# A four-layer graph network on one core: TensorE's updates sent by drains, and GpSimd's gathers issued in pairs behind a count of written ones

## The reference

```python
h = relu(layernorm(x)); x = x + L0(h)   # agg = segment_sum(h[src], dst); MLP 256-512-256, two batch norms
h = relu(layernorm(x)); x = x + L1(h)   # a_in = segment_sum((h@W_in+b)[src]*w, dst)
                                        # a_out = segment_sum((h@W_out+b)[dst]*w2, src); gates: sigmoid, tanh
h = relu(layernorm(x)); x = x + L2(h)   # agg = segment_sum(w*h... [src], dst); MLP 256-256-256, two batch norms
h = relu(layernorm(x)); x = x + L3(h)   # msg = relu([x_i, x_j-x_i]@W1+b1)@W2+b2 per edge; mean over the edges
```

## Time and profile before

| | |
|---|---|
| timed runs, median (lowest to highest) | 3428.49 us (3427.81 to 3428.86) |
| profiled execution, span | 4205.1 us |
| profiled span less timed median | 776.6 us |
| PE matmul busy | 2930.9 us, 70% |
| DVE busy | 2117.9 us, 50% |
| ACT busy | 1141.1 us, 27% |
| POOL busy | 2373.5 us, 56% |
| POOL gathers and scatters, lines 834, 860, 810 and 945 | 1170, 391, 400 and 440 |
| granted TensorE clock, mean | 0.826 |

### The profile page before, as it was taken

One profiled execution on the slowest core, in us unless ns is written; L12 is line 12 of the kernel. 1 busy time (PEld: TensorE's weight loads), 2 busy tenths in 40 slices (PEclk: granted clock), 3 DMA queues, 4 the chain that ended last, 5 costly groups with the idle time before them and its releaser, 6 DMA issues. The chain is left out here.

```text
span 4205.1 us, 55362 instructions
## 1 busy us (share of the span) xinstructions
PE 2930.9 (70%) x11580; PEld 1849.8 (44%) x11581; DVE 2117.9 (50%) x6459; ACT 1141.1 (27%) x3023; POOL 2373.5 (56%) x2458
## 2 busy tenths in 40 slices
PE   3677776555542846677588887755554899988989
PEld 1233333333321434444333332433333548888878
DVE  6566664333320455444456655533333576667664
ACT  1466661000000330000000000300000356666662
POOL 3544445666667046666666666666666226666662
PEclk6788887667665867888799999976676999999999
DMA  3000002333320043333366666433333136666664
GB/s 123 2 1 1 1 1 74 90 89 90 90 56 2 20 139 88 101 106 105 109 176 180 177 176 178 138 89 89 87 91 86 34 124 186 187 188 185 189 187 143
DMA packets 184321, 438.94 MB, mean 104 GB/s; under 512 B 53924, under 2 KB 78623, under 8 KB 184233
## 3 DMA queue, kind: packets, MB, share of 16 engines
q0 software_dynamic: 135568, 372.32, 31.3%
q1 hardware_dynamic: 48665, 65.55, 4.7%
HBM read 403.39 MB, written 34.24 MB: 104 GB/s over the span
## 5 line engine op out<-in xcount | busy, mean ns | idle before, releaser
L834 POOL DMA_INDIRECT acc<-table,stg_idx x1170 | 1128.5, 965 | 767.8 <-issue 349.1
L2116 PE MATMUL psum<-acc,oh 128*128 x2600 | 871.4, 489 | 637.7 <-issue 456.5
L2116 PEld LDWEIGHTS psum<-acc,oh 128*128 128x128 f32 x2600 | 598.2, 244 | 912.3 <-issue 821.2
L1497 DVE TENSOR_TENSOR acc<-acc,psum 128x257 f32 (+1 forms) x660 | 276.0, 418 | 962.7 <-remote 565.4
L1032 ACT CAST stg_idx<-rec 128x2 int32 (+1 forms) x784 | 148.4, 193 | 2113.0 <-remote 841.2
L945 POOL DMA_INDIRECT TT<-qtable,stg_row x440 | 424.1, 964 | 282.4 <-PE psum L2428 150.9
L860 POOL DMA_INDIRECT H<-gtable,stg_idx x391 | 379.1, 970 | 199.5 <-issue 116.5
L2205 PE MATMUL psum<-H 125*128 125x440 bf16 x1600 | 375.5, 399 | 154.2 <-issue 48.2
L2137 PE MATMUL psum<-H,oh 128*128 x880 | 426.2, 630 | 79.8 <-issue 31.1
L810 POOL DMA_INDIRECT recs<-acc,sst_idx x290 | 284.6, 981 | 338.1 <-ACT acc L977 255.6
L2428 PE MATMUL psum<-oh,TT 128*128 128x128 f32 x3520 | 444.3, 277 | 34.7 <-issue 26.0
(11 more groups left out here) (277 smaller groups left out, 3210.7 us busy)
## 6 DMA issues: line engine op xcount, KB each, us to landing
acc<-table,stg_idx POOLq DMA_INDIRECT x1173
TT<-loc_dram SPq DMA_DIRECT2D x22, 320.0 KB
TT<-qtable,stg_row POOLq DMA_INDIRECT x440
Wm<-loc_dram SPq DMA_DIRECT2D x22, 320.0 KB
H<-gtable,stg_idx POOLq DMA_INDIRECT x391
gtable<-H SPq DMA_DIRECT2D x24, 256.0 KB
qtable<-H SPq DMA_DIRECT2D x24, 256.0 KB, 2.2
table<-H SPq DMA_DIRECT2D x8, 640.0 KB
```

The lines of the kernel that those rows point to most:

```text
L834: pool.indirect_dma_start(out=dst[:, c, 0:D], out_offset=None, in_=src, in_offset=bass.IndirectOffsetOnAxis(ap=stg_idx[:, c:c + 1], axis=0 ...
L1497: V.tensor_tensor(at, at, sum_bank(j)[:, 0:w], ALU.add).then_inc(added, 1)
L2116: last = mm(sum_bank(j)[:, 0:w], oh[:, 2 * j + k, :], rows_flat[:, ds(start[j] + k * S, w)], start=(k == 0), stop=(k == 1))
```

## The change

Two things are changed, and each is small in code.

First, TensorE's updates. Where the last matmul of a group of products added to a semaphore, a drain behind it now adds to it. This holds for `used` in the placing phase (400 times), for `summed` in passes 0 to 3 (220 times each) and for `filled` in the four dense stages z0, up0, down0 and back0 (81 times). The other stages' banks, `spread` and pass 4's `summed` stay with the matmul.

Second, GpSimd's gathers of passes 0 to 3. Each of them now also adds one to a new semaphore, `written`, when GpSimd has written its descriptors (`engine_sem`). Before a pair is issued, GpSimd waits until all but the last two of the gathers before it have been written. The scatters have no such wait.

```diff
+WRITES = 2 * (GROUPS - 1) + 1
+BESIDE_SCATTERS = ("z0", "up0", "down0", "back0")
...
+            def pair_before_written(g, n):
+
+                pool.wait_ge(written, g * 2 + (2 - n * (2 * GROUPS - WRITES)))
+                pool.sem_inc(stages_begun, 1)
+
-            def gather_pair(i, j, src, dst):
+            def gather_pair(i, j, n, src, dst):
 
                 pool.wait_ge(staged, i * RING_G + j + 1)
                 pool.sem_inc(stages_begun, 1)
+                pair_before_written(i * RING_G + j, n)
                 for c in (2 * j, 2 * j + 1):
                     pool.indirect_dma_start(
                         out=dst[:, c, 0:D], out_offset=None, in_=src,
-                        in_offset=bass.IndirectOffsetOnAxis(ap=stg_idx[:, c:c + 1], axis=0)
-                    ).then_inc(landed[j], 16)
+                        in_offset=bass.IndirectOffsetOnAxis(ap=stg_idx[:, c:c + 1], axis=0),
+                        engine_sem=written).then_inc(landed[j], 16)
...
+            pool.sem_inc(written, 4)
...
             def done(ins, st, k):
-                ins.then_inc(filled[bank(st, k)], 1)
+                if st in BESIDE_SCATTERS:
+                    nc.tensor.drain().then_inc(filled[bank(st, k)], 1)
+                else:
+                    ins.then_inc(filled[bank(st, k)], 1)
...
-                    last.then_inc(summed, 1)
+                    nc.tensor.drain().then_inc(summed, 1)
...
-                    last.then_inc(used, 1)
+                    nc.tensor.drain().then_inc(used, 1)
```

More of the change, by code:

```diff
@@ L411, in gnn_kernel @@
         stages_begun = sem("stages_begun")
+        written = sem("written")
         zero_filled = sem("zero_filled")
@@ L842, in gathers @@
                     for j in range(RING_G):
-                        gather_pair(i, j, src, dst)
+                        gather_pair(i, j, n, src, dst)
                 for j in range(RING_G - 1):
-                    gather_pair((n + 1) * GITS - 1, j, src, dst)
+                    gather_pair((n + 1) * GITS - 1, j, n, src, dst)
                 pool.wait_ge(staged, (n + 1) * GITS * RING_G)
                 pool.sem_inc(stages_begun, 1)
+                pair_before_written((n + 1) * GITS * RING_G - 1, n)
                 c = 2 * RING_G - 2
@@ L850, in gathers @@
                     out=dst[0:END_ROWS, c, 0:D], out_offset=None, in_=src,
-                    in_offset=bass.IndirectOffsetOnAxis(ap=stg_idx[0:END_ROWS, c:c + 1], axis=0)
-                ).then_inc(landed[RING_G - 1], 16)
+                    in_offset=bass.IndirectOffsetOnAxis(ap=stg_idx[0:END_ROWS, c:c + 1], axis=0),
+                    engine_sem=written).then_inc(landed[RING_G - 1], 16)
             def gather_wide(g, j, half):
@@ L857, in gather_wide @@
                 pool.sem_inc(stages_begun, 1)
+                pair_before_written(g + 2 * GROUPS, 2)
                 r = END_ROWS if half else P
@@ L861, in gather_wide @@
                         out=ring_rows[0:r, c, :], out_offset=None, in_=gtable,
-                        in_offset=bass.IndirectOffsetOnAxis(ap=stg_idx[0:r, c:c + 1], axis=0)
-                    ).then_inc(landed_w[j], 16)
+                        in_offset=bass.IndirectOffsetOnAxis(ap=stg_idx[0:r, c:c + 1], axis=0),
+                        engine_sem=written).then_inc(landed_w[j], 16)
             def gathers_wide():
```

## The result

The changed kernel takes 4319.72 us (median, 4312.87 to 4326.72) against 3428.15 us (3426.13 to 3428.86) of before: a ratio of 1.2604, 95% interval 1.2589 to 1.262. The prediction was 3475.5 us with a range of 3230 to 3550, so the sign was the likelier one and the size was wrong by 844 us.

A forecast was written before the change was run, and what follows sets the result against it. The bound changes by stage: GpSimd's gathers in passes 0 to 3, with TensorE's updates held in the profile but likely not in timed runs. Drains add 33 + 9 + 5 = 47 us to 3428.5, giving 3475.5 us, range 3230 to 3550.

The forecast's parts named there:

- the sign: Whole kernel: slower was given 0.50, same 0.16, faster 0.34.
- Holds at the timed speed: Held TensorE updates beside GpSimd's descriptor trains: likeliest none in the timed runs, so 0 us to gain.
- 667 us of holds: Holds summed in the profiled execution: passes 338 us, late scatters 132, placing 197.
- The rival with real holds: Holds also exist in timed runs, so the change ends faster: 3268 us in the middle, 3085 at the end; chance 0.34.
- The argument that a recording makes them: Holds read as mainly a cost of being profiled: 0.70 us steps on idle register operations, timed runs 776.6 us shorter.
- The `written` wait: GpSimd's wait before each gather pair in passes 0 to 3: covered by the pair before, 0 us.
- Drains in the placing phase: 400 drained columns: TensorE's column grows from 0.73 to 0.90 us against VectorE's 0.816, costing 33 us, bounds 0 to 72.
- 1.1 dear: Marker for the profile after: placing columns 0.9 us apart as forecast, 0.82 for covered drains, 1.1 for dear ones.
- Around the late scatters: Drains on 56 banks of up0, down0 and z0 at 0.166 us each: 9 us, upper bound 21.
- Drains on sums: 220 drains per pass: 0 us in passes 0, 1 and 3, 5 us in pass 2, bounds 0 and 13.
- 1.19 us per gather: GpSimd's most per gather in timed runs; 8.9 gathers make 10.6 us per iteration, against TensorE's 11.1 with drains in pass 2.
- drains are dear, TensorE becomes the bound: Rival: a drain of 0.40 us costs 191 us over placing, pass 2 and late scatters, 3620 us; chance 0.09.

The follow-up runs named there:

- r1: The kernel before, unchanged, run and profiled again for a second trace: 3428.61 us, span 3426.9 us.
- v2: The changed kernel with the updates of the sums in passes 0 to 3 back on their matmuls, all else kept: 3623.32 us, ratio 1.056.
- s1: The kernel before with a drain behind each of the 880 sums of passes 0 to 3, nothing else: 4118.61 us, ratio 1.2023.
- v1: As s1, plus ten unread 128x128 matmuls at the start of each iteration in passes 0 and 3: 3846.31 us, ratio 1.1215.
- s4: The kernel before with a drain behind only the fifth sum of each iteration in passes 0 to 3: 3443.79 us, ratio 1.005.
- s3: The kernel before with a drain behind sums 1 to 4 of each five in passes 0 to 3: 3815.27 us, ratio 1.1135.
- e3: The kernel before with drains behind only the 81 banks of z0, up0, down0 and back0: 4281.09 us beside 4260.53, ratio 1.0053.
- s: Group of four runs with drains or halts on the sums of passes 0 to 3; the before beside them took 3428.07 us.
- t: Group of four runs (sums with filler, placing drains, `written` wait, drains on even columns); the before beside them took 4267.84 us.

## Why the prediction was wrong, step by step

- **Holds at the timed speed: 0.** Right (r1), and with it the bound: passes near 495 us each. The 667 us of holds are real differences between the two traces of before: 336 us in the passes, 135 around the late scatters, 218 in the placing phase, and 84 in pass 4 that the sum had left out. The rival with real holds (0.34) fell. The argument that a recording makes them fell too: the 0 is right, its reason was wrong, and the agreement is in part luck. No run shows what makes the steps of 0.70 us: the register operations of line 2137 are at 3 to 709 ns in the first trace of before and at 46, smallest and largest alike, in r1's. Profiled, r1 took 3428.61 us, no more than the seven runs of before beside it (3428.66 to 3431.28).
- **The `written` wait: 0.** Right: 0.30 us before each gather in v2.
- **Drains in the placing phase: 33 us, bounds 0 to 72.** 171 measured. The step that failed is what followed from "A drain ends the overlap, since nothing behind it starts before the tail is over". The sentence holds, and the 0.90 us with it (each of the 400 drains ends 20 to 23 ns behind the last matmul's recorded end in the changed kernel's trace), but as a price it is incomplete: I counted the 166 ns tail and at most a weight load. Behind the drain stand the column's register operation, its wait and the issue of its first load as well, 0.32 us that used to be done ahead. The column of 1.22 us is beyond the "1.1 dear" of my markers.
- **Around the late scatters: 9 us, at most 21.** 21 measured in v2, the same omission: four banks of up0 are 9.8 us apart from the next four, where r1 has 7.7.
- **Drains on sums: 5 us in pass 2, 0 elsewhere.** 217, and 94, 158 and 184 elsewhere (s1). This is the term that broke the forecast, and it failed twice. "In passes 0, 1 and 3 TensorE has time to spare", put at 0, took the idle time of the earlier trace rows as free. Part of it was where the sequencer prepared the next sums, two register loads of 1.24 us an iteration among it, and behind a drain none of the loads ran beside matmuls in passes 0 and 3 (0 us of them in the changed kernel, 34 and 36 of 95 in r1). In pass 2, by its rows, this is most of the loss, though no run sets it apart. And the step took TensorE's clock as given: in pass 3 the share granted fell from 0.74 to 0.51, and v1, with the same drains and a clock of 0.99, loses 2 us there instead of 184. For pass 1 the shares of the two stay open. The sum for pass 2 also had GpSimd's side too short: the 1.19 us per gather from the room in the timed runs is 1.26 in r1, so its limit is 11.2 us an iteration and not 10.6; by the prediction's own 11.1 for TensorE its 5 us would have been 0.
- **The rival "drains are dear, TensorE becomes the bound"** (0.09, 3620 us) had the right mechanism. It priced a drain at 0.40 us, where a column of the placing phase grew by 0.49 (0.73 to 1.22), but counted no register loads, no clock, and only 25 iterations of one pass. With 0.5 us a sum and 3.0 us of bare loads its 10.3 us would have come to 15.8, pass 2's 16.

## What to carry to other kernels

Ahead of putting a drain into TensorE's stream, list all that its sequencer does between two pieces of work, register loads first: here that list (0.32 to 0.52 us, up to 3.8 with two register loads), and not the matmul's tail of 166 ns alone, is what the drains laid bare. Add it to TensorE's work, and compare that serial iteration with the engine that sets the pace: in s4, whose iteration stayed under it in passes 0 and 3, the drains there cost nothing. Do the sum at a granted clock of 0.50 too (a sum took 2.07 us there, 1.13 at 1.00), since drains behind sums 1 to 4 went with a granted clock of 0.51 and 0.52 in pass 3 (s1, s3), where r1 has 0.74 and s4 0.78. And if the profiled span differs from the timed median by a fifth, get a trace at the timed speed before reading causes out of it.

## What the runs showed of the hardware

- One kernel, two speeds: 3428 and 4260 us, each steady within a set of runs (3425 to 3432, and 4246 to 4277), each with profiles as long as the times (the first trace of before, 4205, lies near the second). At 4260 updates of TensorE are held beside long trains of GpSimd's descriptors, drained or not (beside the late scatters ScalarE takes its banks 11.1 us apart in the first trace of before and 11.2 in e3, against 1.7 in r1). What chooses between them stays open; it isn't the recording alone and isn't this code, since the same kernel was profiled without holds in r1. Both speeds are on record with chip number 2 (before at 3428 beside s, at 4268 beside t).
- Useless matmuls in the bare stretches gave back 272 us (s1 to v1): the granted clock of the two passes was 1.00 and 0.99 instead of 0.71 and 0.51.
- Long bare stretches did not by themselves go with the low clock: s4's pass 3, with a drain and some 3.7 us bare behind every fifth sum, had 0.78, while s3's, drained behind the other four sums, had 0.52. Which of the spaces set it, and how, stays open.
- A drain behind four back-to-back matmuls of 440 columns ended 20 to 23 ns behind the last one's recorded end (changed kernel, all 400); what it kept waiting behind it, 0.32 to 0.52 us of sequencer work and up to 3.8 us with register loads, was the larger part of its price: a column grew by 0.49 us, of which 0.32 were bare.
